# A two-layer graph convolution beside a four-layer mixer: the passage between its layers one FFN group later, and its last part among the experts

## The reference, cut to what matters

```python
edge_index = jnp.stack([src, dst])                      # 53125 edges, sorted by dst, 3125 nodes
xn = _layernorm(x)                                      # 3125 x 256
x = x + _L0_gnn_ref(xn, edge_index, edge_type, ...) + _L0_mix_ref(xn, ...)
x = x + _L0_ffn_ref(_layernorm(x), ...)                 # shared MLP + top 2 of 4 experts
# _L0_gnn_ref, twice:
m = x[src] * rel[edge_type]
m = concat([m[:half] @ W_in, m[half:] @ W_out])
agg = segment_sum(m * norm[dst][:, None], dst)
h = h + res * tanh(agg + h @ W_loop + b)                # at the end: h @ mu_w + mu_b
# _L0_mix_ref, four layers:
x = x + linear_attention(layernorm(x))
x = x + gelu(layernorm(x) @ W1 + b1) @ W2 + b2          # 256 -> 1024 -> 256
```

## Time and profile before

| what | value |
|---|---|
| median of 3 executions | 1974.16 us (1971.7 to 1982.78) |
| the profiled execution | 1972.02 us |
| its span (first to last instruction) | 1970.3 us |
| PE busy | 1732.7 us (88%) |
| POOL busy | 1312.5 us (67%) |
| DVE busy | 1225.8 us (62%) |
| ACT busy | 628.8 us (32%) |

### The profile page before, as it was taken

How to read it: one execution, slowest core, us unless ns; L and a number is a source line. 1 busy time by engine, 2 the same in 40 slices (tenths; PEclk the granted TensorE clock), 3 DMA queues, 4 the chain that set the end, 5 groups by cost and what they waited for, 6 DMA issues and landing times.

```text
span 1970.3 us, 29281 instructions
## 1 busy us (share of the span) xinstructions
PE 1732.7 (88%) x9388; PEld 1300.7 (66%) x9388; DVE 1225.8 (62%) x3354; ACT 628.8 (32%) x1552; POOL 1312.5 (67%) x1303
## 2 busy tenths in 40 slices
PE   3889799998899999989987689977988898889999
PEld 2456577775587777667765466644666676667998
DVE  6785465565756566665646558576655565644766
ACT  4542243343324333422423123321121121213433
POOL 6777777777777777777777757766776776650000
PEclk9999899999999999989999899987999999988999
DMA  9677666667766766876678865665665666560000
GB/s 273 195 216 239 198 192 206 188 196 244 226 202 189 212 194 192 250 231 205 203 212 251 253 216 180 209 210 182 214 200 167 189 199 204 169 154 13 15 27 28
DMA packets 194577, 371.47 MB, mean 189 GB/s; under 512 B 37993, under 2 KB 126095, under 8 KB 194430
## 3 DMA queue, kind: packets, MB, share of 16 engines
q0 software_dynamic: 77632, 223.91, 39.6%
q1 hardware_dynamic: 92228, 126.68, 19.4%
q10 hardware_dynamic: 24570, 19.04, 3.3%
HBM read 305.39 MB, written 64.95 MB: 188 GB/s over the span
## 4 chain that ended last, share of the span: by engine, by line
PE 44%; POOL 28%; issue 11%; DVE 11%; DMA 3%; SPq 1%; ACT 1%; DVEq 1%; ACTq 0%; POOLq 0%
POOL xg L984 16%; POOL rg L931 12%; PE ps_down L2830 9%; PE ps_hid L2818 8%; PE ps_kv L3149 3%; PE ps_seg L2683 3%; PE ps_hid L3298 2%; PE ps_x L561 2%; PE ps_seg L2692 2%; PE ps_kv L2727 2%; PE ps_x L2782 2%; DVE xg L1087 2%; DVE acc L1065 1%; PE ps_hid L3289 1%; DMA xg<-h_rows,idx_tab 1%
## 5 line engine op out<-in xcount | busy, mean ns | idle before, releaser
L984 POOL DMA_INDIRECT xg<-h_rows,idx_tab x416 | 426.9, 1026 | 182.5 <-issue 118.5
L984 POOL DMA_INDIRECT xg<-xn_rows,idx_tab x416 | 430.4, 1035 | 129.4 <-issue 124.9
L931 POOL DMA_INDIRECT rg<-relation_rows,idx_tab x416 | 419.5, 1009 | 133.7 <-issue 126.4
L1087 DVE TENSOR_TENSOR xg<-xg,rg 128x512 f32<-128x512 f32 x416 | 280.8, 687 | 188.0 <-DMA rg<-relation_rows,idx_tab 161.5
L2818 PE MATMUL ps_hid<-hT,wff 128*128 128x250 f32 (+1 forms) x1920 | 374.1, 346 | 2.5 <-ACT hT L2240 1.8
L2830 PE MATMUL ps_down<-wff,gT 128*125 128x256 f32 x1600 | 375.8, 389 | 0.0
L2818 PEld LDWEIGHTS ps_hid<-hT,wff 128*128 128x128 f32 x1920 | 314.9, 192 | 51.5 <-issue 21.2
L2830 PEld LDWEIGHTS ps_down<-wff,gT 128*125 128x125 f32 x1600 | 304.5, 194 | 45.4
L2254 ACT ACTIVATE gT<-ps_hid,b1p 128x250 f32<-128x250 f32 (+1 forms) x480 | 177.2, 433 | 258.2 <-PE ps_hid L2818 258.0
L2683 PE MATMUL ps_seg<-xg,hot 128*32 128x257 f32 x1664 | 138.2, 406 | 46.2 <-DVE xg L1087 46.1
L1065 DVE SCALAR_TENSOR_TENSOR acc<-ps_seg,in_tile,acc 125x257 f32 x208 | 100.4, 483 | 98.9 <-PE ps_seg L2692 69.3
(11 more groups left out here) (397 smaller groups left out, 2578.4 us busy)
## 6 DMA issues: line engine op xcount, KB each, us to landing
second_relation_rows<-rg SPq DMA_DIRECT2D x104, 512.0 KB, 4.0
rg<-second_relation_rows SPq DMA_DIRECT2D x104, 512.0 KB, 4.0
wff<-L_mix_W ACTq DMA_DIRECT2D x8, 1024.0 KB, 7.0
rg<-relation_rows,idx_tab POOLq DMA_INDIRECT x416
xg<-xn_rows,idx_tab POOLq DMA_INDIRECT x416
xg<-h_rows,idx_tab POOLq DMA_INDIRECT x416
h_rows<-qT_all SPq DMA_DIRECT2D x25, 112.0 KB
qrow<-h_rows ACTq DMA_DIRECT2D x25, 112.0 KB
```

Of the source, the lines that this page charges most:

```text
L931: pool.indirect_dma_start(rg[:, k, :], None, rel_d, bass.IndirectOffsetOnAxis(ap=idx_tab[:, step, 1:2], axis=0))\
L984: pool.indirect_dma_start(xg[:, k, 0:D], None, rows, bass.IndirectOffsetOnAxis(ap=idx_tab[:, step, 0:1], axis=0))\
L1087: dve.tensor_tensor(m, m, r, ALU.mult).then_inc(s_msg, 1)
```

## The change

The order of work is changed, and the buffers are arranged so that it can be. What is computed stays.

- DENSE_GROUP is 4: the passage stands in (2,3). The steps are spread anew: 20 to 24 a group before it, 44 in (2,4), 58 to 60 a group in layer 3, and STEPS_TAIL = 40 among the experts of the first tiles (`tail_marks`: four steps, twice a tile).
- PIECE_LAG is 15: a slot of the second layer's dense part runs 15 slots later, one and a half groups. `slots_of` gives the slots of each turn s of the tail: one in each of the first seven, then two.
- Layer two's relation rows use half of `rg` (16 steps, as `xg`; before 32), and the experts' weights stand in the other half from the third joint on. ACT issues these loads.
- The experts use other PSUM banks, as `ps_seg` is still in use: layer 3's product goes to a half of `ps_kv` for the first four tiles, beside the slots' mu product in the same bank. `rows_free` makes PE wait before a slot until DVE has read it; `add_experts` comes a turn later.
- `add_x` is issued earlier, and DVE's mu addition waits for it, instead of the other way round.

```diff
-STEPS_GROUP = ((20, 26, 24, 24, 24), (20, 24, 24, 24, 22), (18, 24, 68, 48, 54), (58, 58, 58, 56, 48))
+STEPS_GROUP = ((20, 24, 22, 22, 20), (18, 22, 22, 22, 20), (18, 22, 24, 66, 44), (58, 60, 60, 60, 58))
+STEPS_TAIL = 40
-DENSE_LAYER, DENSE_GROUP = 2, 3
+DENSE_LAYER, DENSE_GROUP = 2, 4
+PIECE_LAG = 15
+TAIL_EDGES = 5
...
+        FIRST_SLOT, ONE_SLOT = NG * 2 * GT - PIECE_LAG, 7
+        def slots_of(s):
+            if s < ONE_SLOT:
+                return (FIRST_SLOT + s,), ()
+            at = FIRST_SLOT + 2 * s - ONE_SLOT
+            return ((at,), (at + 1,)) if at < 2 * (NB + 2) else ((), ())
+        def tail_marks(s):
+            n = STEPS_TAIL // UNIT
+            return [min(-(-n * k // (2 * TAIL_EDGES)), n) for k in (2 * s + 1, 2 * s + 2)]
...
-            with sp.Fori(0, STEPS2 // (2 * RING)) as it:
+            with sp.Fori(0, STEPS2 // RING) as it:
                 for b in range(len(s_r2ld)):
-                    sp.wait_ge(s_msg, it * (2 * RU) + (UNITS + RU + 1 + (b + 1) * BU - 2 * RU))
+                    sp.wait_ge(s_msg, it * RU + (UNITS + 1 + (b + 1) * BU))
...
             def add_x(gi):
                 pool.wait_ge(s_xr, NG * L + gi + 1)
-                pool.wait_ge(s_emz, (gi + 1) * GT)
...
+            def rows_free(s):
+                t = s - FIRST_SLOT - 3
+                if t >= 0 and beside_edges(t):
+                    pe.wait_ge(s_ez, t + 2)
...
                     def aside(s):
                         if lay == L - 1:
-                            dense_beside(gi * (2 * GT) + s, split_tile)
+                            dense_beside(gi * (2 * GT) + s - PIECE_LAG, split_tile)
...
-            for s in range(1, NT + 2):
+            upto = edges.stage(at_tail)
+            for s in range(NT + 2):
                 if s < NT:
                     shared_1(s)
+                upto(marked[0])
+                for u in sooner:
+                    dense_beside(u, split_tile)
...
+                for u in later:
+                    dense_beside(u, split_tile)
                 if 1 <= s <= NT:
                     layer_2(s - 1)
                 turn(3)
+                upto(marked[1])
                 if s > 1:
                     layer_3(s - 2)
```

More of the change, by code:

```diff
@@ L993, in _ @@
                     pool.memset(acc[:, :, :], 0.0).then_inc(s_azero, 1)
-            for gi in range(ADD_BESIDE, NG):
-                add_x(gi)
         @block.vector
@@ L1583, in iteration @@
                     n.add_b2()
-                early()
                 aside(8)
@@ L2651, in _ @@
                 turned(2)
-                if s == 1:
-                    dense_beside(behind + 3)
-                if s <= NT:
+                for u in later:
+                    dense_beside(u)
+                if 1 <= s <= NT:
                     hidden_2(s - 1)
```

234 lines of the change are left out of this document (127 added, 107 removed).

## The result

The changed kernel takes 1995.63 us (median of 4 runs, 1993.34 to 1996.54), the kernel before in the same session 1973.34: a ratio of 1.0104 [1.0081, 1.0127], 1% slower. The profiled execution took 1993.34 us for a span of 1991.4.

A forecast was written before the change was run, and what follows sets the result against it. It took POOL's gathers to pace the first half while PE had room, and POOL to stand still at the end. Experts' start 1701.5 plus tail 235.4 gave a span of 1937, forecast 1938 us; range 1906 to 1970.

The forecast's parts named there:

- The front's first half: Up to the passage: its group starts at 1008, 30 of 50.4 us PE idle taken back; passage begins at 1069.
- As long as it is not held (it may lead by 16 steps, and I count 12 to 13 at most), its last gather is again at 1131: End of layer one: POOL gathers on unheld, and the passage ends 28.7 us after its last gather, at 1160.
- By the work alone, PE's 88.3 us, it ends at 1157: Passage: PE's busy time alone, counted from its begin at 1069, as a second estimate of its end.
- 67.6: Front's gain in us: (2,4) starts at 1161 instead of 1228.6.
- my rival on the other side: Front not paced by gathers, moved group and passage simply add: 1999 us, decided below a 34 us front win; chance 0.05.
- (2,4) to the experts: (2,4) 67.5 and joint 71.0 us, (3,0) with (3,1) 143, then 84, 88.5, 86.5: experts start at 1701.5.
- ACT's loads: Start of (3,0): 13 loads at 0.434 us, 5.6 us ahead of the first gelu; PE feels some 2.
- The tail: From the experts' start to the end: 174.0 + 24.3 slots + 8.6 steps + 28.5 waits and slower PE = 235.4 us.
- The term of 40 steps at 0.21: Tail: PE's price for the edge steps among the experts, 8.6 us with the last placement.
- The slots' 1.62: Tail: PE's price in us for each of 15 added slots, 24.3 us in all.
- The waits of `rows_free`: Tail, turns 3 to 6: PE held until `add_experts`, 3.8 us a turn, 15 in four.
- The ring: Layer two's relation loads lead by 16 steps, not 32: hidden; rival if not, 52 us more, 1990 us; chance 0.05.

The follow-up runs named there:

- e5_among: Changed kernel with 20 edge steps of (2,3) given back to earlier groups and 16 of 40 among the passage's tiles moved ahead of it: 1991.9 us, 1.0086.
- e15: Changed kernel with lag 5, no tail steps, last edge sums added before the experts, `add_x` 16 steps sooner, front steps of e5_among: 1982.1 us, 1.0070.
- e1_spread: Changed kernel with 20 of the 66 edge steps of (2,3) given back to the ten groups ahead of it: 1993.3 us, 1.0087.
- e16: Changed kernel with the edits of e5_among, e2_third and e3_lag9, and the next tiles' norm two turns sooner in the tail: 1967.9 us, 0.9976.
- e17: e16 with the third layer's rows in two places in turn from tile 13 on: 1969.4 us, 0.9976.
- e13: Changed kernel with passage back in (2,2), lag 5, edge steps as before the change (none in the tail), `add_x` 16 steps sooner: 1999.3 us, 1.0138.
- e2_third: Changed kernel with the experts' third layer of the first four tiles in `ps_dn`, so slots no longer wait for the addition of the experts' rows: 1981.7 us, 1.0039.
- e3_lag9: Changed kernel with `PIECE_LAG` 9 instead of 15, six slots back from the tail into layer 3: 1984.6 us, 1.0042.
- e10_lag_only: Changed kernel with passage back in (2,2), no tail steps, 286 steps in layer 3; lag 15 and shorter ring stay: 2006.9 us, 1.0152.

## Why the prediction was wrong

- **The front's first half came out by two errors that cancel.** The passage begins at 1077.0, less the prologue's 5.1 (215.8 for 210.7) 1072, for 1069. But its group started at 1019 so counted, for 1008: of the 50.4 us idle PE took back 10 (40.8 are left), not 30. The first part then took 52.5 us for 61, with 0.4 idle, where the passage's group of before had 10.3.
- **"As long as it is not held (it may lead by 16 steps, and I count 12 to 13 at most), its last gather is again at 1131": this step failed, and it is the large one.** POOL was held for 35.2 us, and the last gather came 36 late. I had counted a lead of before, where POOL was the pacer: gathers started less steps summed are 9 to 12 there at the starts of the groups (1,0) to (2,2). With 22 steps fewer they are 12 to 16 at the same places, and between them the ring is full.
- **"By the work alone, PE's 88.3 us, it ends at 1157": this failed too**, and e5_among shows that it alone would have been enough: its last gather is at 1136.9, and the passage still takes 101 us, of which PE works 82. With POOL not held the front wins 39 us (e5_among) to 47 (e15: (2,4) at 1181.5), not 67.6; in the changed kernel it won 32.2. The changed kernel's front is below the 34 at which my rival on the other side decides, and its 1999 is near what came. Of its mechanism one half is shown: the passage kept its length (119.4 for 118.6). The other half isn't: ahead of it the gathers do pace, as e1_spread's idle time says.
- **(2,4) to the experts: 540.5 for 538.8, by two errors that cancel.** (2,4) and the joint took 120.6, not 138.5: I priced (2,4) by the (2,3) of before, 68.7 us, though its own row had 320 products for the 378 of that one; it took 56.3, of which PE was busy 54.4. (3,0) and (3,1) took 162.1, not 143: I let POOL's lead pay for 12 of the 118 steps, and it ended the stretch as far ahead as it began it (13 and 12 steps, gathers started less steps summed). 120 operations at 1.35 are the 162. And layer 3 alone varies by 6 us between kernels with the same work in it, so that the sum came within 2 us is luck.
- **ACT's loads** took 7.8 us, 0.60 each and not 0.434. PE felt 2.10 us of them, as the forecast's "some 2" had it:

```profile
1320.87 0.40 ACTq L796 DMA_DIRECT2D rg<-L_ffn_sW  x1
...
1327.80 0.87 ACTq L806 DMA_DIRECT2D bo_b<-L_ffn_eb  x1
1328.78 1.28 ACT L2286 ACT_TABLE_LOAD   x1 [12.48 <-PE ps_hid L2852]
```

```profile
1331.04 2.84 PE L2852 MATMUL ps_hid<-hT,wff 128*128 128x250 f32 x8 [2.10 <-ACT gT L2286]
```

  But that is the lowest value of the eighteen kernels that have these loads. The thirteen take 7.8 to 11.8 us there, and PE then waits 2.1 to 9.0 for the first gelu with the passage in (2,3), 7.4 to 11.3 with it in (2,2); in the kernel before it does not wait for it. No run put the loads elsewhere.
- **The tail: the waits were mis-sized, not the slots.** It grew by 82.2 us for the forecast's 61.4. PE's busy time in it grew by 46.3 (forecast 38.4), its idle time by 35.9 (forecast 23). The term of 40 steps at 0.21, 8.6 us, measures 25.1, as PE waits for each unit of them. The slots' 1.62 was right: 1.66 by ten of them in turns 7 to 13. The waits of `rows_free`, 15 us in turns 3 to 6, measure 9.5 beside the edge steps, 7.2 of it in turn 6; without steps, the bank and the late edge sums together are 20.6. The order of norm and third layer, 6 to 9 us by the tails of e16 and e17, was in no term: I had read the diff of the turn for what came in, not for what went later. The sum: 25.1 for the steps, 37.2 for ten slots with the bank and the late sums, and 18.8 (e13's tail against the one before, with five slots and the order of the norm), 81 of the 82.2 us.
- **The ring held.** No wait of any engine for layer two's relation rows stands in the nineteen traces; its loads land in 4.0 us. It was not run by itself.
- **Open:** what keeps e13's layer 3 at 432.1 us with five slots fewer than before (426.6). Three waits that the kernel before lacks or has smaller stand in it: PE's 7.4 us for the first gelu, behind the loads; POOL's 27.9 for `add_x`; PE's 31.7 for the mu addition (26.3 before). No run turned the order of `add_x` back, or took the loads away. Nor is it settled why e5_among, e2_third and e3_lag9 don't add.

Of what the change was to bring, then: the moved group gives 49 us up to (3,0), and 50 steps more in layer 3 take them back at about 1 us each; at shorter lags 0.6% of it stays. The tail steps win 9 to 13 us by the medians. What costs is the lag with all that came in with it, 1.5% (e10_lag_only), and the count of late slots is not the main part of that: with five of them in place of fifteen 1.4% are left (e13, with waits of its own making). Of the rest the runs price the order of the norm, 6 to 9 us, and, in the tail, bank and late sums, 20.6; the loads and `add_x` they do not price.

## What to carry to other kernels

A producer that paces a stage stops doing so when the stage is given less of its product: then its ring fills, and what it could have done in that time is lost, so work moved past a pacer must be checked for the lead at each place. When a wait is removed, ask for the next chain at the same place, and don't price it from the busy time of one engine in it (88 us for what took 101). A transfer moved up in an in-order queue can hold all that stands behind it (`add_x` in e13: 27.9 us). And a diff of a queue's order must be read for what moved later behind its consumer too, not only for what was added.
